# Token shift in front of the feed-forward by on-chip transfers, with new orders and banks, in a gated four-layer network on one Trainium2 core

## The chip, the cores and the metric

The kernel runs on one core of one Trainium2 chip. The metric is the time of one execution on the device in microseconds (us). The engines are TensorE (PE in the profile, its weight loads PEld), VectorE (DVE), ScalarE (ACT), GpSimd (POOL), and SyncE (SP), which issues all transfers here.

## The reference

Sixteen sequences of 128 tokens by 128 features go through four blocks of attention and feed-forward, each added with a gate. The change concerns the feed-forward of the first block, itself a transformer of six layers with local attention. One layer, for one sequence x (128 x 128):

```
x  = x + attention(shift_tokens(x))
x  = x + ffn(shift_tokens(x))
shift_tokens(t): columns 0 to 63 as they are; columns 64 to 127 of row i come from row i-1, and row 0 gets zeros

attention: qkv = x @ Wqkv (128 x 3072); 16 heads of 64
           q, k = l2norm(q) * q_scale, l2norm(k) * k_scale; both rotated by tables (cos, sin, a scale)
           scores of each window of 32 queries against its own and the previous window, times 8
           mask, softmax, @ v, @ Wo (1024 x 128)
ffn:       xn = layernorm(x) * g + b
           a, gate = split(xn @ W1 + b1)        (each 341 wide)
           (a * gelu(gate)) @ W2 + b2
```

## The kernel before

The file is written engine by engine: each engine runs its own list of instructions, in order, and waits on semaphores. Nothing is planned at run time; the orders are written out by hand.

A unit is one sequence in one layer, 6 x 16 = 96 units. Tokens lie on the 128 partitions. `local_transformer` (L445) runs three units at once in a software pipeline: each call of an engine's `stages(a, b, c)` does the first part of unit a, the middle of unit b, which is the one before, and the feed-forward of unit c, the one before that. The calls alternate between two sets of buffers (s = 0, 1). A layer is a loop of seven passes with two calls each and two calls written out behind it; between layers GpSimd also builds the rotary tables (`rotary_factors`, L1645).

The parts of a unit, in the order of its own dependences:

- `tokens` (VectorE, L2136) copies the sequence from Y to xw. `tokens_T` (TensorE, L786) transposes it, and ScalarE's `shifted` (L1299) copies the result to xsT with the shift, which is along the free dimension there.
- `queries_keys` j = 0 to 3 (L795): queries in j = 0, 1, keys in j = 2, 3, each a 128 x 512 result that fills a bank of PSUM. `values` (L816) likewise, in two halves. ScalarE squares each of the four (`squares`, L1313), VectorE sums the squares by head (`square_sums`, L2143, `floors`, L2151) and multiplies each of the four by the rotary tables (`rotated`, L2162 and L2164, two instructions). ScalarE makes inverse norms by logarithm and exponential (L1337, L1345). GpSimd adds the two products (`rotary_sum`, L1665) and multiplies by the inverse norms (`normalised`, L1679).
- `queries_keys_T` (L809, four transposes for each j) and ScalarE's copy; `scores` m = 0, 1 (L843, 64 small records each), `masked` (VectorE, L2184), `maxima` (L2192), `differences` (GpSimd, L1687), `exponentials` (ScalarE), `probs_T` (L857) and its copy, `probs_values` (L880).
- `middle_values` (SP, L532): four transfers inside on-chip memory that lay out the values for the third window.
- `inverse_sums` (L2202), `outputs` (L2209), `outputs_T` (L890), `project` (L900), `first_residual` (VectorE, L2214), which gives y1.
- `shift_back` (TensorE, L905): y1 multiplied by the identity (columns 0 to 63) and by a shift matrix (columns 64 to 127) into PSUM. `shifted_stats` and `statistics` (L2218, L2223), GpSimd's `token_var` and `token_std` (L1696, L1700), `shifted_normed` (L2227), `normed_T` (L915), `up` (L922), `gelu`, `hidden` (L2237), `down` (L934), `biased` (GpSimd, L1692), `second_residual` (L2244), which writes Y.

ScalarE loads a table of functions twice in each call, for exponentials and for the gelu. PSUM has eight banks, given to these results by the lists `lb_...` (L245 to L248); where two results share a bank, the second waits until the first is read.

## Time and profile before

| | |
|---|---|
| runs before | 2669.9, 2675.39, 2679.36 us, median 2675.39 |
| profiled execution | 2678.02 us; span from its first to its last instruction 2676.1 us |
| mean granted TensorE clock | 0.979 |
| engines busy, share of the span | TensorE 94%, weight loads 72%, VectorE 74%, ScalarE 66%, GpSimd 56% |
| instructions | 103018 |
| first L786 of the local transformer to its last | 144.0 to 1839.9 us |

The profile records one execution. A group of matmuls in order of time is merged to one row with its count: an fp32 matmul leaves two records, a transpose one. The ends of matmuls are modelled, and consecutive ones overlap in the records, so the distance from one block's start to the next block's start is what the block takes when nothing waits. Idle time in brackets is that of the engine in front of the row, with what released it.

### The profile page before, as it was taken

To read this page: it belongs to the slowest core of one execution; us is meant where nothing else is said; L and a number is where in the kernel's file an instruction comes from. 1 tells how busy PE (TensorE), PEld (TensorE's weight loads), DVE (VectorE), ACT (ScalarE), POOL (GpSimd) and SP (SyncE) were. 2 spreads that over 40 slices of the span, in tenths; PEclk is the share of its full clock that TensorE was granted. 3 is DMA by queue.
4 is the path that set the end of the run, shared out by engine and by line. 5 is a ranking of instruction groups with operands and counts; after the bars stand their busy time and mean duration, and the time that the engine had idled before them with its cause. 6 is when DMAs were issued, how large, how long until landed. Compare 5 with 4: busy or idle time off the path is not lost.

```text
span 2676.1 us, 103018 instructions
## 1 busy us (share of the span) xinstructions
PE 2507.1 (94%) x41090; PEld 1932.3 (72%) x41090; DVE 1977.9 (74%) x4815; ACT 1762.2 (66%) x3794; POOL 1492.9 (56%) x1917
## 2 busy tenths in 40 slices
PE   7879999999999999999999999999898978999898
PEld 5647677777767767777677767776677966899667
DVE  5777888888778788878788888887466877465564
ACT  5567777777777777777777777777344356333465
POOL 4567667666766766676667666775232146000472
PEclk9989999999999999999999999999799989899999
DMA  2200000111001100110011000000002000000022
GB/s 85 72 14 14 14 16 18 28 29 29 18 22 32 32 14 22 32 29 21 18 32 29 23 18 18 16 14 15 4 4 85 0 5 5 1 0 1 12 76 79
DMA packets 56280, 66.72 MB, mean 25 GB/s; under 512 B 25097, under 2 KB 30932, under 8 KB 55380
## 3 DMA queue, kind: packets, MB, share of 16 engines
q1 hardware_dynamic: 56148, 64.87, 8.7%
q8 instruction: 93, 1.52, 0.2%
q14 instruction: 39, 0.32, 0.0%
HBM read 38.23 MB, written 1.05 MB: 15 GB/s over the span
## 4 chain that ended last, share of the span: by engine, by line
PE 80%; DVE 6%; issue 5%; POOL 4%; ACT 3%; DVEq 1%; SPq 0%; POOLq 0%; DMA 0%; ACTq 0%
PE ps L795 13%; PE ps L900 6%; PE ps L816 6%; PE ps L809 6%; PE ps L880 5%; PE ps L843 5%; PE ps L922 4%; PE ps L857 3%; PE ps L1014 3%; PE ps L934 3%; PE ps L890 3%; PE ps L998 3%; PE ps L999 3%; ACT area L1190 2%; PE ps L738 2%
## 5 line engine op out<-in xcount | busy, mean ns | idle before, releaser
L1190 ACT ACTIVATE area<-ps 128x512 f32<-128x512 f32 (+3 forms) x1520 | 758.1, 532 | 415.9 <-PE ps L786 130.0
L1665 POOL TENSOR_TENSOR area<-area 128x512 f32<-128x512 f32 x384 | 482.2, 1277 | 7.9 <-DVE area L2164 7.9
L1687 POOL TENSOR_TENSOR area<-area,mx 128x512 f32<-128x512 f32 x192 | 200.2, 1043 | 491.1 <-DVE mx L2192 491.1
L795 PE MATMUL ps<-lw,area 128*128 128x512 f32 x768 | 414.1, 622 | 1.1 <-ACT area L1190 0.7
L1679 POOL TENSOR_TENSOR area<-area,rnq 128x512 f32<-128x512 f32 x384 | 393.2, 1046 | 7.5
L1313 ACT ACTIVATE area<-ps 128x512 f32<-128x512 f32 x384 | 227.4, 592 | 88.7 <-PE ps L795 88.6
L2162 DVE TENSOR_TENSOR area<-ps,table 128x512 f32<-128x512 f32 x384 | 261.0, 680 | 8.2 <-ACT area L1313 5.4
L2164 DVE TENSOR_TENSOR area<-ps,table 128x512 f32<-128x512 f32 x384 | 261.5, 681 | 0.0
L2143 DVE TENSOR_REDUCE ssq<-area 128x8 f32<-128x512 f32 x384 | 252.3, 677 | 2.4 <-ACT area L1313 1.5
L809 PE MATMUL ps<-ident,area 128*128 128x128 f32 x1536 | 218.6, 275 | 11.1 <-POOL area L1679 7.7
L809 PEld LDWEIGHTS ps<-ident,area 128*128 128x128 f32 x1536 | 180.7, 142 | 66.3 <-issue 54.3
L900 PE MATMUL ps<-lw,area 128*128 128x128 f32 x1536 | 210.2, 280 | 0.7 <-ACT area L1190 0.7
L1428 ACT ACTIVATE area<-ps 128x256 f32<-128x256 f32 x208 | 79.4, 384 | 198.8 <-PE ps L999 198.7
L880 PEld LDWEIGHTS ps<-area 64*32 64x32 f32 x9216 | 134.3, 105 | 89.7 <-issue 89.7
L900 PEld LDWEIGHTS ps<-lw,area 128*128 128x128 f32 x1536 | 186.4, 191 | 5.6 <-ACT area L1190 0.9
L816 PE MATMUL ps<-lw,area 128*64 128x512 f32 x768 | 186.0, 605 | 0.0
L843 PEld LDWEIGHTS ps<-area 64*32 64x32 f32 x12288 | 134.2, 106 | 58.7 <-issue 47.2
L2184 DVE TENSOR_TENSOR area<-ps,band_f 128x512 f32<-128x512 f32 x192 | 131.9, 687 | 59.4 <-PE ps L843 59.4
L922 PEld LDWEIGHTS ps<-xnT,lw 128*128 128x128 f32 (+1 forms) x1152 | 139.9, 180 | 48.1 <-ACT xnT L1190 46.1
L880 PE MATMUL ps<-area 64*32 64x65 f32 x9216 | 165.6, 225 | 1.2 <-issue 0.7
L843 PE MATMUL ps<-area 64*32 64x64 f32 x12288 | 165.3, 225 | 0.0
L880 PE MATMUL ps<-lvm,area 64*32 64x65 f32 x3072 | 154.0, 225 | 0.0
(301 smaller groups left out, 5681.9 us busy)
## 6 DMA issues: line engine op xcount, KB each, us to landing
lvm<-area SPq DMA_DIRECT2D x384, 65.0 KB
lw<-in_wqkv SPq DMA_DIRECT2D x36, 256.0 KB
area<-in_moe_w SPq DMA_DIRECT2D x24, 256.0 KB, 2.8
lw<-in_wout SPq DMA_DIRECT2D x12, 256.0 KB
ctxT<-in_ctxT SPq DMA_DIRECT2D x64, 38.5 KB, 1.8
lw<-in_moe_w SPq DMA_DIRECT2D x8, 256.0 KB, 2.8
lw<-in_wff SPq DMA_DIRECT2D x6, 341.0 KB
lw<-in_moe_g SPq DMA_DIRECT2D x1, 1152.0 KB
```

The costliest lines, as they stand in the source:

```text
L795: nc.tensor.matmul(banks[:, lb_qk[j], :], xsT[s], wqkv[w.p][:, j * 512:(j + 1) * 512], start=True, stop=True).then_inc(l_qk_ps, 1)
L809: last = nc.tensor.transpose(banks[:, lb_qkT[j], c * S:(c + 1) * S], QR[s][:, j * 512 + c * 128:j * 512 + (c + 1) * 128], ident[:, :])
L816: last = nc.tensor.matmul(banks[64 * odd:64 * odd + 64, lb_v[j], :].rearrange("p (c e) -> p c e", e=LD), xsT[s][:, 64 * j:64 * j + 64], he ...
L843: last = nc.tensor.matmul(banks[out_rows, lb_scores[m][odd], c * 64:(c + 1) * 64].rearrange("p (b n) -> p b n", n=WINDOW), QKT[s][64 * odd ...
L880: last = nc.tensor.matmul(banks[out_rows, lb_pv[m][odd], c * 65:(c + 1) * 65], LPT[s][rows, at:at + 32], v, start=True, stop=True)
L900: last = nc.tensor.matmul(banks[:, lb_project, 0:D], LOT[s][:, c, :], wout[w.p][:, c, :], start=(c == 0), stop=(c == 7))
L1190: return nc.scalar.activation(dst, src, ACT.Identity if kw else ACT.Copy, **kw)
L1665: pool.tensor_tensor(QR[s][:, cols], QR[s][:, cols], RA[s][:, cols], ALU.add).then_inc(l_rsum, 1)
L1679: pool.tensor_tensor(rows, rows, rnq[s][:, 8 * j:8 * j + 8, None].to_broadcast([S, 8, LD]), ALU.mult).then_inc(l_qkn, 1)
L2143: V.tensor_reduce(ssq[s][:, 8 * j:8 * j + 8], blk(SQ[s], j), AX.X, ALU.add).then_inc(l_ss, 1)
L2162: V.tensor_tensor(blk(RA[s], j), src, factors[:, 0:1, :].to_broadcast([S, 8, LD]), ALU.mult)
L2164: V.tensor_tensor(blk(QR[s], j).rearrange("p h (k e) -> p h k e", k=2), other, factors[:, 1:2, :].to_broadcast([S, 8, LD]).rearrange("p h ...
```

## The change

The shift in front of the feed-forward is done by SP: as soon as y1 of a unit is written, one transfer inside on-chip memory copies rows 0 to 126 of its columns 64 to 127 to rows 1 to 127 of 64 further columns beside it (`ysh`, whose row 0 there is set to zero once). `shifted_stats` and `shifted_normed` read the columns 0 to 63 and 128 to 191 of `ysh`. The two matmuls of `shift_back`, the shift matrix and its load go, so one load less is counted in `w1_loaded`. SP's list gets the pipeline's form. All four compute engines have a new order within `stages`, and results have other banks. The keys and queries j = 1, 3 come first, then 2 and 0; on TensorE the units' scores stand at the head of the call.

```diff
-        yb = [part(s, at_ + 1024, D) for s in bufs]
+        ysh = [part(s, at_ + 896, D + 64) for s in bufs]
+        yb = [part(s, at_ + 1088, D) for s in bufs]
...
-        lb_tokens, lb_qk, lb_qkT, lb_v = 3, (4, 3, 4, 0), (3, 0, 2, 5), (1, 5)
-        lb_scores, lb_probs, lb_pv = ((1, 2), (1, 2)), (5, 4), ((2, 3), (2, 3))
-        lb_outputs = (7, 4)
-        lb_project, lb_shift, lb_xnT, lb_up, lb_down = 7, 7, 0, (6, 7), 6
+        lb_tokens, lb_qk, lb_qkT, lb_v = 7, (3, 4, 0, 6), (4, 7, 3, 3), (2, 3)
+        lb_scores, lb_probs, lb_pv = ((6, 7), (5, 6)), (1, 4), ((4, 5), (6, 7))
+        lb_outputs = (5, 6)
+        lb_project, lb_xnT, lb_up, lb_down = 5, 1, (1, 2), 1
...
+            def shifted_tokens(s, unit):
+                sp.wait_ge(l_y1, unit + 1)
+                sp.dma_start(ysh[s][1:S, D:D + 64], y1[s][0:S - 1, 64:D]).then_inc(l_sh_ps, 16)
+            def stages(a, b, c):
+                if a:
+                    middle_values(*a)
+                    shifted_tokens(*a)
...
```

TensorE's waits that are new, and its order (b is the middle unit):

```diff
             def queries_keys(s, w, j):
                 if j == 0:
+                    follow(pe, l_v, nth(0, w.it, s, 2, 1) - 2)
...
+                if j == 3:
+                    follow(pe, l_masked, nth(0, w.it, s, 2, 1) - 2)
...
             def scores(s, w, m):
...
+                    follow(pe, l_y1, nth(0, w.it, s) - 1)
...
             def stages(a, b, c):
-                if b: queries_keys_T(*b, 1)
-                if c: shift_back(*c)
-                if a: tokens_T(*a)
-                if b: scores(*b, 0)
-                if a: queries_keys(*a, 0)
-                if b: queries_keys_T(*b, 3)
-                if a: queries_keys(*a, 1)
-                if c: normed_T(*c, b)
-                if b: scores(*b, 1)
-                if a: queries_keys(*a, 2)
...
+                if b:
+                    scores(*b, 1)
+                    queries_keys_T(*b, 2)
+                if a: tokens_T(*a)
+                if b:
+                    queries_keys_T(*b, 0)
+                    values(*b, 1)
+                    scores(*b, 0)
+                if a:
+                    queries_keys(*a, 1)
+                    queries_keys(*a, 3)
+                if c: normed_T(*c)
+                if a:
+                    queries_keys(*a, 2)
+                    queries_keys(*a, 0)
+                if b:
+                    probs_T(*b, 1, a)
+                    probs_T(*b, 0)
+                if a: values(*a, 0)
+                if b:
+                    probs_values(*b, 0)
+                    probs_values(*b, 1, a)
+                if c:
+                    up(*c, 0)
+                    up(*c, 1, a)
+                if b:
+                    outputs_T(*b, 0)
+                    outputs_T(*b, 1)
+                if a: queries_keys_T(*a, 1)
+                if b:
+                    project(*b, 0)
+                    project(*b, 1)
+                if a: queries_keys_T(*a, 3)
+                if c:
+                    down(*c, 0)
+                    down(*c, 1)
+                    down(*c, 2)
```

The new orders of the others, each shown whole in the sequence of one call (a, b, c as above):

```
ScalarE: b qkT 3, b qkT 2, a shifted, b qkT 0, load exp table, b values 1, a squares 1, b exponentials 1,
         a squares 3, c normed_T, b exponentials 0, a squares 2, b probs_T 1, b probs_T 0, a squares 0, a values 0,
         a logs and inverse norms 1, then 0, load gelu table, b outputs_T 0, c gelu 0, b outputs_T 1, c gelu 1, 2, a qkT 1
GpSimd:  b rotary_sum 1, 3, b normalised 1, 3, b rotary_sum 0, 2, b normalised 2, 0,
         c biased, c token_var, c token_std, b differences 1, 0
VectorE: a tokens, b masked 1, c shifted_stats, c statistics, b maxima 1, c shifted_normed, b masked 0, b maxima 0,
         a rotated 1, 3, a square_sums 3, 2, 1, a floors 1, a square_sums 0, b inverse_sums 0, a floors 0,
         b inverse_sums 1, b outputs 0, 1, a rotated 0, 2, c hidden 1, 0, b first_residual, c hidden 2, c second_residual
```

```diff
             def tokens(s, w):
+                follow(dve, ffn_done, nth(0, w.it, s) + G - 3)
                 follow(dve, l_y1, nth(0, w.it, s) - 2)
...
+            def shifted_tokens(s):
+                return ysh[s].rearrange("p (k n) -> p k n", n=64)[:, 0:3:2, :]
             def shifted_stats(s, w):
-                dve.wait_ge(l_sh_ps, nth(0, w.it, s))
-                V.bn_stats(st[s][:, 0:6], banks[:, lb_shift, 0:D]).then_inc(l_st, 1)
+                dve.wait_ge(l_sh_ps, 16 * nth(0, w.it, s))
+                V.bn_stats(st[s][:, 0:6], shifted_tokens(s)).then_inc(l_st, 1)
...
             def shifted_normed(s, w):
-                V.tensor_scalar(xn[s][:, :], banks[:, lb_shift, 0:D], mv[s][:, 0:1], rs[s][:, 0:1],
+                V.tensor_scalar(xn[s][:, :].rearrange("p (k n) -> p k n", n=64), shifted_tokens(s), mv[s][:, 0:1], rs[s][:, 0:1],
```

## Rows read from the trace of the kernel before

**Rows 1.** Windows: us; busy of PE, PEld, DVE, ACT, POOL; clock; DMA share; GB/s.

```profile
144.00:1839.90 1695.90, 1657.49 (x32346) 1193.96 (x32347) 1364.48 (x2922) 1305.27 (x2644) 1159.11 (x1257) 1.00 0.09 22
...
751.00:772.00 21.00, 20.88 (x350) 15.12 (x350) 14.32 (x32) 13.88 (x28) 11.13 (x12) 0.84 0.03 8
...
1255.44:1272.87 17.43, 17.43 (x344) 12.66 (x345) 14.01 (x31) 13.77 (x28) 11.43 (x13) 1.00 0.05 12
1237.07:1255.44 18.37, 17.57 (x347) 12.66 (x346) 15.06 (x32) 13.83 (x28) 12.92 (x14) 1.00 0.12 25
```

**Rows 2.** TensorE in order of time: start us, us, line, tiles, count, idle before.

```profile
1268.33 0.49 PE L934 MATMUL ps<-lw,area 85*128 85x128 f32 x2
1268.65 1.06 PE L900 MATMUL ps<-lw,area 128*128 128x128 f32 x8
...
1272.38 0.43 PE L907 MATMUL ps<-area,ident 128*128 128x64 f32 x2
...
1272.87 0.30 PE L786 MATMUL ps<-ident,xw 128*128 128x128 f32 x1
1273.10 0.86 PE L843 MATMUL ps<-area 64*32 64x64 f32 x64
1273.90 1.11 PE L795 MATMUL ps<-lw,area 128*128 128x512 f32 x2
1274.85 0.60 PE L809 MATMUL ps<-ident,area 128*128 128x128 f32 x4
1275.28 1.02 PE L795 MATMUL ps<-lw,area 128*128 128x512 f32 x2
...
1278.10 1.49 PE L922 MATMUL ps<-xnT,lw 128*128 128x128 f32 x12
...
1281.61 1.94 PE L816 MATMUL ps<-lw,area 128*64 128x512 f32 x8
```

**Rows 3.** TensorE in time at back edge and layer boundary; L786's waits (us, times).

```profile
1255.43 0.32 PE L786 MATMUL ps<-ident,xw 128*128 128x128 f32 x1 [0.80 <-DVE xw L2136]
...
1288.13 0.66 PE L809 MATMUL ps<-ident,area 128*128 128x128 f32 x4 [0.57 <-POOL area L1679]
...
  DVE xw L2136: 37.2, 32
```

**Rows 4.** VectorE's and GpSimd's timelines around two token copies.

```profile
1254.33 0.98 DVE L2136 TENSOR_SCALAR xw<-Y 128x128 f32 x1 [0.41 <-DVE area L2214]
...
1272.48 0.23 DVE L2136 TENSOR_SCALAR xw<-Y 128x128 f32 x1 [0.16 <-DVE area L2214]
...
1254.18 1.04 POOL L1679 TENSOR_TENSOR area<-area,rnq 128x512 f32<-128x512 f32 x1
...
1272.59 1.04 POOL L1679 TENSOR_TENSOR area<-area,rnq 128x512 f32<-128x512 f32 x1
```

**Rows 5.** VectorE in order of time: sums, outputs, a rotation, a mask.

```profile
1268.43 0.21 DVE L2202 RECIPROCAL rc<-ps 128x8 f32<-128x8 f32 x1
1268.68 0.69 DVE L2209 TENSOR_TENSOR area<-ps,rc 128x512 f32<-128x512 f32 x1
1269.28 0.68 DVE L2162 TENSOR_TENSOR area<-ps,table 128x512 f32<-128x512 f32 x1
...
1274.13 0.69 DVE L2184 TENSOR_TENSOR area<-ps,band_f 128x512 f32<-128x512 f32 x1 [0.47 <-PE ps L843]
```

**Rows 6.** GpSimd in order of time: three sums, and the power.

```profile
1264.52 3.75 POOL L1665 TENSOR_TENSOR area<-area 128x512 f32<-128x512 f32 x3
...
1274.01 0.55 POOL L1700 TENSOR_TENSOR rs<-ve,neghalf 128x1 f32<-128x1 f32 x1
```

**Rows 7.** Transfers: an issue in time; then KB each, us from issue to landing.

```profile
1271.78 0.51 SPq L537 DMA_DIRECT2D lvm<-area  x1
...
shift<-in_shift SPq DMA_DIRECT2D x1, 64.0 KB, 1.8
...
lw<-in_moe_w SPq DMA_DIRECT2D x8, 256.0 KB, 2.8
```

More of the change, by code:

```diff
@@ L96, in program @@
         Y = sb("Y", [S, B, D])
[L97 removed]
+        ident = sb("ident", [S, S])
         band_f = sb("band_f", [S, 2 * WINDOW])
@@ L519, in _ @@
             behind = [(dst[:, :], dram[name], w1_loaded) for dst, name in (
-                (shift, "shift"), (band_f, "band"), (heads2, "heads2"), (rank, "rank"), (aff1, "aff1"), (moe1_r, "moe1_r"))]
+                (band_f, "band"), (heads2, "heads2"), (rank, "rank"), (aff1, "aff1"), (moe1_r, "moe1_r"))]
             behind += [(dst[:, :, :], dram[name], w1_loaded) for dst, name in ((rot, "rot"), (w1, "w1"), (moe1_gu, "moe1_gu"), (moe1_d, "moe1_d"))]
-            behind[8:8] = [(dst, src, lw_loaded[p]) for p in range(2) for part in layer_parts(p, p) for dst, src in part]
+            behind[7:7] = [(dst, src, lw_loaded[p]) for p in range(2) for part in layer_parts(p, p) for dst, src in part]
             per = -(-len(behind) // (IT - 1))
@@ L538, in middle_values, with three @@
                     sp.dma_start(LVM[s][at + 32:at + 64, :, :], LV[s][at + 32:at + 64, 0, :, :]).then_inc(l_vm, 16)
-            def layer(l):
-                with sp.Fori(0, IT) as pr:
-                    for s in range(G):
-                        middle_values(s, l * B + pr * G + s)
+            def shifted_tokens(s, unit):
[5 more added lines that the diff above has]
+                    shifted_tokens(*a)
+            def three(s, unit):
+                stages((s, unit), (1 - s, unit - 1), (s, unit - 2))
             def layer_and_next_weights(l, p):
@@ L554, in layer_and_next_weights @@
                             sp.dma_start(dst, src).then_inc(lw_loaded[p], 16)
-            layer(0)
+            stages((0, 0), None, None)
+            stages((1, 1), (0, 0), None)
+            with sp.Fori(0, IT - 1) as pr:
+                for s in range(G):
+                    three(s, pr * G + G + s)
             with sp.Fori(0, DEPTH // 2 - 1) as lp:
@@ L559, in _ @@
                 layer_and_next_weights(lp * 2 + 2, 1)
-            layer(DEPTH - 1)
+            with sp.Fori(0, IT) as pr:
+                for s in range(G):
+                    three(s, (DEPTH - 1) * B + pr * G + s)
+            stages(None, (1, DEPTH * B - 1), (0, DEPTH * B - 2))
+            stages(None, None, (1, DEPTH * B - 1))
             contexts(1)
@@ L2247, in stages @@
                 if a: tokens(*a)
+                if b: masked(*b, 1)
                 if c:
@@ L2250, in stages @@
                     statistics(*c)
-                if b: masked(*b, 0)
+                if b: maxima(*b, 1)
                 if c: shifted_normed(*c)
-                if b: maxima(*b, 0)
+                if b:
+                    masked(*b, 0)
+                    maxima(*b, 0)
+                if a:
+                    rotated(*a, 1)
+                    rotated(*a, 3)
+                    square_sums(*a, 3)
+                    square_sums(*a, 2)
+                    square_sums(*a, 1)
+                    floors(*a, 1)
+                    square_sums(*a, 0)
+                if b: inverse_sums(*b, 0)
+                if a: floors(*a, 0)
+                if b:
+                    inverse_sums(*b, 1)
+                    outputs(*b, 0)
+                    outputs(*b, 1)
                 if a:
                     rotated(*a, 0)
-                    square_sums(*a, 1)
-                    rotated(*a, 1)
-                if b: masked(*b, 1)
-                if a:
-                    square_sums(*a, 0)
-                    floors(*a, 0)
-                if b: maxima(*b, 1)
-                if c: hidden(*c, 0)
-                if b: inverse_sums(*b, 0)
-                if a: rotated(*a, 2)
+                    rotated(*a, 2)
                 if c:
                     hidden(*c, 1)
+                    hidden(*c, 0)
+                if b: first_residual(*b)
+                if c:
                     hidden(*c, 2)
-                if b: outputs(*b, 0)
-                if a:
-                    square_sums(*a, 3)
-                    square_sums(*a, 2)
-                    floors(*a, 1)
-                if b:
-                    inverse_sums(*b, 1)
-                    outputs(*b, 1)
-                if a: rotated(*a, 3)
-                if c: second_residual(*c)
-                if b: first_residual(*b)
+                    second_residual(*c)
             def mixture(m):
```

266 lines of the change are left out of this document (123 added, 143 removed).

## The prediction

> **What bounds the kernel now.** I read the busy time of the engines first, then the windows, then one unit of the local transformer engine by engine in order of time. By the page TensorE is the busiest engine, at 94% of the span. The changed stage runs from the first token transpose at 144.0 us to the last at 1839.9: 1695.9 us for 95 intervals, 17.85 each, with TensorE busy 98% of it, VectorE 80% and GpSimd 68% [rows 1]. Before and behind the stage nothing is touched but one load. Two kinds of unit make the 17.85. A clean one takes 17.43 us and has no TensorE gap; the one before it takes 18.37 with 0.8 us less busy than long [rows 1]. In the clean one each block starts as soon as the one before has streamed: a block of four transposes lasts 0.60 us and the next starts 0.43 behind its start [rows 2]. There TensorE's own work sets the pace, and a block's slot is its duration less some 0.16. The 0.94 us of the other is one wait, of the token transpose for xw [rows 3], and the next view says why: the copy of the tokens (L2136) took 0.98 us there and 0.23 in the clean unit. In the slow case it started 0.15 us after a GpSimd multiplication and ended with it, 0.09 us behind; in the clean one the copy came first by 0.11 us [rows 4]. That happened at the back edge of the loop over pairs, where VectorE starts the copy 0.41 us behind the residual's end and not 0.16 [rows 4]. There are 6 x 6 back edges; the transpose waited for xw 32 times, 37.2 us in all with the pipeline's start [rows 3]. I take 30 x 0.94 = 28 us. The rest of the excess over 95 x 17.43 = 1656 is about 6 us at five layer boundaries, where the new rotary tables make GpSimd late for the transposes (0.57 us at the first block of them [rows 3]), and about 6 us at one place, where the granted clock fell to a mean of 0.84 for 21 us [rows 1]. 1656 + 28 + 12 = 1696.
>
> **What the change removes.** shift_back, two matmuls of four records: from its start to the next block 0.49 us [rows 2]. TensorE alone would then need 17.43 - 0.49 = 16.94. The orders are new too, and a block behind one of another shape, or behind a wait, costs 0.03 to 0.1 more than behind its like (the same query/key product lasts 1.11 behind the scores and 1.02 behind transposes, slots of 0.95 and 0.86 [rows 2]). Adding the blocks in the new order at their shorter starts-to-starts gives 16.6; I keep 16.5 to 16.9 as TensorE's floor. The shift matrix's load (64 KB) went beside the first stage and gives nothing.
>
> **What it adds and moves, in one unit.** Times are from u, the start of the feed-forward's up products. TensorE behind u: up 1.32, two output transposes 0.88, transposes (a,1) 0.44, project 1.80, transposes (a,3) 0.44, down 0.78, so the next stage's scores(b,1) start at 5.7 (up is 1.49 less 0.16, a half of project 1.06 less 0.16, down four records like transposes and two more, 0.33); scores 0.80, transposes (b,2) 0.44, tokens 0.23: transposes (b,0) could start at 7.2 [rows 2]. They need GpSimd's last product, and GpSimd waits for VectorE. VectorE reads the second probability product at u+0.1 (a hand-over like that from xw's end, 1255.31, to TensorE at 1255.43 [rows 3, 4]); from there it is 0.25 to outputs and then steps of 0.60 [rows 5]: outputs at 0.35 and 0.95, rotated(a,0) at 1.55 and 2.15, rotated(a,2) at 2.75 and 3.35, done at 4.05. GpSimd's sum(2) starts at 4.15 and takes 1.25 [rows 6], normalised(b,2) and (b,0) 1.04 each [rows 4] from 5.45: 6.5, done at 7.55. So transposes (b,0) start at 7.65, 0.45 late. Before, three of the four rotations stood early and one sum and one product behind the last; now the chain of two rotations, sum and two products is the bound. From there to the next u: 0.44, a half of the values 0.93, scores 0.80, two query/key products 1.81, normed 0.20, two more 1.78, probabilities' transposes 0.90, values 0.93 [rows 2], and the two probability products, as many small blocks as the scores, 1.59: 9.4. One more wait in it: queries_keys(a,3) now takes the bank of scores(b,0), so masked(b,0) (0.69 behind a hand-over of 0.24) [rows 2, 5] must fit under one product of 0.95: 0.05 to 0.1. A clean unit is 7.65 + 9.4 + 0.1 = 17.15 us, 0.28 below now. The new waits sit at the head of what is queued: behind transposes (b,0) wait all scores and products of the stage, and the masks behind those.
>
> **The transfer.** SP waits for y1 of its unit, then issues one DMA of 127 rows x 256 bytes. SP has four of its own a unit (0.51 us to issue [rows 7]) some 10 us earlier, and the next layer's weights follow behind, so nothing is ahead of it. No row has an on-chip transfer's landing. Loads of as many rows took 1.8 us (64 KB) and 2.8 (256 KB) [rows 7]; below lies the issue alone, 0.5. I take 2.0, near the 64 KB load, which is the nearest in rows and size. y1 ends at u+4.9, the rows are there at 7.0. VectorE gets to shifted_stats only behind masked(b,1), at 7.35: hidden, with 0.35 to spare. Then aggregation to 7.95, GpSimd's variance and power to 8.85 [rows 6], and masked(b,0), which cannot start before 10.05, is due after shifted_normed.
>
> shifted_normed reads and writes on-chip memory now, as the token copy does. If it goes as the copy does, it is held by a GpSimd operation that has begun: differences(b,1) starts at 8.85, as soon as the power ends, shifted_normed 0.07 behind it, and so ends 0.08 behind a 1.04 us operation [rows 4], at 9.97 and not at 9.2. That is still ahead of 10.05 and free. The Trainium skill ("SBUF — State Buffer", Who interferes with whom) has the rule: a tensor_scalar between SBUF operands can take the port pair that VectorE shares with GpSimd, exclusively, and whichever issues first makes the other block. The trace agrees for the copy [rows 4]; for shifted_normed, which read PSUM until now, no row can say. By that page the step is held; without it the step is shorter than now; the sum is the same either way, so long as 10.05 stands.
>
> **The token copy** decides the rest. second_residual starts at S+0.2 (S is the start of scores(b,1), u+5.75), the copy at S+0.65 = u+6.4. normalised(b,2) runs from 5.5 to 6.5: the copy is held to 6.6 and does no harm, since the token transpose stands behind transposes (b,2). At a back edge it starts up to 0.25 later [rows 4], 6.5 to 6.65, when normalised(b,0) has begun: held to 7.65, token transpose 7.75, transposes (b,0) at 8.0 and not 7.65 (0.35), and masked(b,1) and the statistics start 0.8 late, so that shifted_normed ends at 10.8 and masked(b,0) holds queries_keys(a,3) 0.4. Together 0.75. The rotary tables cost nothing at layer boundaries now: GpSimd has both first sums done 2 us before the inverse norms come, so the 6 us go.
>
> Sum, against the profiled span of 2676.1 (the run took 2678.0, the runs' median is 2675.4; the gain is taken from the median): 95 x 17.15 = 1629, the clock's place 6, 36 back edges x 0.75 = 27: 1662 against 1696. Gain 34, **2641 us**.
>
> **Rivals.**
> No collision at the edges (the margin is 0.1 us, my hand-overs are no better): 1635, gain 61, 2614. For it: some 6 of the 36 edges go free of it today already, with the same list of instructions.
> The GpSimd chain is hidden after all and TensorE's floor sets the pace (16.7): 95 x 16.7 + 6 = 1593, gain 103, 2572. For it: TensorE is at 98% now. Against: the chain above is 0.45 too long by rows that repeat to 0.01.
> Collision in every unit: the copy at u+6.4 need only slip 0.15 against GpSimd, then 95 x 17.9 + 6 = 1706, 2686, slower by 0.4%. It is the page's port rule at its worst; rows 4 show the price.
> The transfer's landing is on the path (ends slower): place, bn_stats in front of masked(b,0). Up to 2.4 us it is free; each further us moves the power, shifted_normed and masked(b,0), and so queries_keys(a,3), by one. At 3.1 us a unit is 17.8 and the gain is gone; at 4.0 it is 18.7, +83 us, 2758. For it: 128 rows in 256 KB took 2.8; against: 64 KB took 1.8, and this is 32 KB.
>
> **Chances.** Edges collide 0.36, none 0.27, every unit 0.14, floor 0.08, transfer late or another wait of that kind 0.15 (a third of it mild, still a gain). The likeliest is 2641, by itself 2628 to 2660. The range reaches from the side without collisions to the one with all, 2600 to 2686: that leaves out the floor and most of the late transfer. What this kernel's measurement tells from no change is about 0.3%, 8 us: faster 0.36 + 0.27 + 0.08 + 0.03 = 0.74, within 0.11, slower 0.15.
>
> **What would show it.** TensorE records a unit 340 and not 344. Waits of TensorE on GpSimd's L1679 at transposes (b,0), near 0.45 us in each unit: if none, the floor rival holds. The token copy's mean near 0.3 in odd units and 0.9 at edges, or long everywhere. shifted_normed at about 1.05 us, held, or 0.25. Period 17.15 between edges, 17.9 at them. Layer boundaries no longer visible. bn_stats waiting for a DMA would show the late transfer. The prediction is wrong if the period's floor is off the 17.15, that is, if VectorE reaches the rotations later than I think (squares on ScalarE late behind the table load), which would push everything: 0.2 us a unit are 19 us.

## The result and the profile after

After the change the kernel takes 2722.77 us (median of four runs, 2718.56 to 2726.48) where the kernel before, on the same chip, takes 2674.39 (2669.9 to 2679.36): a ratio of 1.0177, interval 1.0154 to 1.0199. It is 48 us slower, and the prediction said 34 us faster.

The windows view of the kernel after, for the whole changed stage and for one unit (columns as in [rows 1]):

```profile
143.73:1884.44 1740.71, 1639.37 (x32031) 1153.26 (x32031) 1418.18 (x2923) 1291.09 (x2644) 1167.80 (x1258) 0.99 0.09 23
1264.46:1282.61 18.15, 17.26 (x341) 12.19 (x341) 14.81 (x32) 13.61 (x29) 12.27 (x14) 1.00 0.10 25
```

The stage took 1695.9 us before and takes 1740.7 now, 18.32 a unit. TensorE works 18 us less and waits 63 more. The chain of waits says for what, in its piece from first_residual (L2236) of one unit to the query/key product (L810) behind it: start, us, what.

```profile
1334.79 0.30 DVE area L2236
1335.10 0.02 issue
1335.11 3.37 DMA area<-area
1338.49 0.02 issue
1338.51 0.31 DVE st L2243
...
1338.91 0.19 DVE mv L2248
...
1339.17 0.19 POOL ve L1715
...
1339.44 0.56 POOL rs L1719
1340.00 0.03 issue
1340.03 0.06 DVE xn L2252
1340.08 0.92 issue
1341.00 0.69 DVE area L2206
1341.69 0.04 issue
1341.74 1.12 PE ps L810 x2
```

The transfer (DMA area<-area) lands 3.37 us behind its issue, not 2.0 (3.37 to 3.73 over all 96 units, median 3.42). Everything behind it is a chain: bn_stats (L2243), aggregation, GpSimd's variance and power, shifted_normed (L2252), and behind that masked(b,0) (L2206), which frees the bank that queries_keys(a,3) takes. The timelines of the same stretch: VectorE, GpSimd and TensorE.

```profile
1338.51 0.30 DVE L2243 BATCH_NORM_STATS2 st<-area 128x6 f32<-128x128 f32 x1 [1.00 <-DMA area<-area]
...
1340.03 1.06 DVE L2252 TENSOR_SCALAR xn<-area,mv,rs 128x128 f32<-128x128 f32 x1 [0.36 <-POOL rs L1719]
1341.00 0.68 DVE L2206 TENSOR_TENSOR area<-ps,band_f 128x512 f32<-128x512 f32 x1
```

```profile
1339.96 1.04 POOL L1706 TENSOR_TENSOR area<-area,mx 128x512 f32<-128x512 f32 x1
```

```profile
1339.16 0.85 PE L863 MATMUL ps<-area 64*32 64x64 f32 x64
1339.93 1.12 PE L810 MATMUL ps<-lw,area 128*128 128x512 f32 x2
1341.74 1.12 PE L810 MATMUL ps<-lw,area 128*128 128x512 f32 x2 [0.68 <-DVE area L2206]
```

VectorE waits 1.00 us for the transfer, and shifted_normed takes 1.06 us, ending 0.09 behind the GpSimd multiplication (L1706, differences(b,1)) that runs beside it. The scores that masked(b,0) reads ended at 1340.01; it starts at 1341.00. TensorE's two pairs of L810 stand 1.81 apart where 0.95 would do. The waits view (engine, tile, line, what for: us, times, longest) says that this is every unit:

```profile
DVE st L2243 <- DMA area<-area: 57.5, 95, 2.2
PE ps L810 <- DVE area L2206: 63.1, 93, 1.0
```

### The profile page after: what moved, and what is told of

Its sections match the earlier page's. It is cut to its first block, busy times and chain, and to the rows that moved or that the text cites. A ratio compares the mean times of both kernels' runs of the same rounds, so it can differ in the third digit from the quotient of the medians.

```text
span 2722.5 us, 102526 instructions
## 1 busy us (share of the span) xinstructions
PE 2487.4 (91%) x40706; PEld 1890.1 (69%) x40706; DVE 2032.2 (75%) x4815; ACT 1747.6 (64%) x3794; POOL 1500.6 (55%) x1919
## 3 DMA queue, kind: packets, MB, share of 16 engines
HBM read 38.16 MB, written 1.05 MB: 14 GB/s over the span
## 4 chain that ended last, share of the span: by engine, by line
PE 62%; DMA 12%; DVE 10%; issue 7%; POOL 5%; ACT 3%; DVEq 0%; POOLq 0%; SPq 0%; ACTq 0%
DMA area<-area 12%; PE ps L810 10%; PE ps L920 7%; PE ps L937 6%; PE ps L900 6%; PE ps L833 4%; PE ps L910 3%; PE ps L877 3%; PE ps L1031 3%; PE ps L1015 3%; PE ps L1016 3%; DVE area L2206 2%; POOL rs L1719 2%; PE ps L824 2%; ACT area L1207 2%
## 5 line engine op out<-in xcount | busy, mean ns | idle before, releaser
L1207 ACT ACTIVATE area<-ps 128x512 f32<-128x512 f32 (+3 forms) x1520 | 769.2, 531 | 500.5 <-PE ps L824 244.4
L810 PE MATMUL ps<-lw,area 128*128 128x512 f32 x768 | 392.8, 622 | 63.9 <-DVE area L2206 63.1
L810 PEld LDWEIGHTS ps<-lw,area 128*128 128x128 f32 x768 | 124.0, 191 | 226.7 <-DVE area L2206 141.1
L1706 POOL TENSOR_TENSOR area<-area,mx 128x512 f32<-128x512 f32 x192 | 200.1, 1042 | 146.7 <-DVE mx L2214 146.5
L2165 DVE TENSOR_REDUCE ssq<-area 128x8 f32<-128x512 f32 x384 | 244.4, 678 | 8.4
L824 PE MATMUL ps<-ident,area 128*128 128x128 f32 x1536 | 238.3, 278 | 4.6 <-POOL area L1698 4.5
L833 PE MATMUL ps<-lw,area 128*64 128x512 f32 x768 | 208.5, 621 | 0.8
L920 PE MATMUL ps<-lw,area 128*128 128x128 f32 x1536 | 194.9, 280 | 0.0
L824 PEld LDWEIGHTS ps<-ident,area 128*128 128x128 f32 x1536 | 175.1, 142 | 15.4 <-POOL area L1698 6.5
L920 PEld LDWEIGHTS ps<-lw,area 128*128 128x128 f32 x1536 | 178.7, 192 | 5.2 <-ACT area L1207 0.3
L937 PE MATMUL ps<-xnT,lw 128*128 128x128 f32 (+1 forms) x1152 | 158.1, 288 | 4.9 <-issue 4.3
L900 PE MATMUL ps<-area 64*32 64x65 f32 x9216 | 156.5, 225 | 2.3 <-issue 2.2
```

What stands on the lines that cost most here:

```text
L810: nc.tensor.matmul(banks[:, lb_qk[j], :], xsT[s], wqkv[w.p][:, j * 512:(j + 1) * 512], start=True, stop=True).then_inc(l_qk_ps, 1)
L824: last = nc.tensor.transpose(banks[:, lb_qkT[j], c * S:(c + 1) * S], QR[s][:, j * 512 + c * 128:j * 512 + (c + 1) * 128], ident[:, :])
L833: last = nc.tensor.matmul(banks[64 * odd:64 * odd + 64, lb_v[j], :].rearrange("p (c e) -> p c e", e=LD), xsT[s][:, 64 * j:64 * j + 64], he ...
L900: last = nc.tensor.matmul(banks[out_rows, lb_pv[m][odd], c * 65:(c + 1) * 65], LPT[s][rows, at:at + 32], v, start=True, stop=True)
L920: last = nc.tensor.matmul(banks[:, lb_project, 0:D], LOT[s][:, c, :], wout[w.p][:, c, :], start=(c == 0), stop=(c == 7))
L937: last = nc.tensor.matmul(banks[0:hi - lo, lb_up[value], c * S:(c + 1) * S], wff1[w.p][:, at:at + hi - lo], xnT[s][:, :], start=True, stop ...
```

## The experiments

Each median stands beside runs of the kernel before on the same chip (2675.3 to 2676.3); ratios are to those. "Stage" is the distance from the first token transpose to the last, read as in the windows.

**The transfer without its last row**, so that 126 and not 127 rows move (the last token's shifted half is left out).

```diff
-sp.dma_start(ysh[s][1:S, D:D + 64], y1[s][0:S - 1, 64:D])
+sp.dma_start(ysh[s][1:S - 1, D:D + 64], y1[s][0:S - 2, 64:D])
```

> The changed kernel with one row less in the token transfer: 126 rows instead of 127 (the second half of the last token's row is not moved, so it stays what it was). Theory A: the transfer lands late (3.4 us from issue, where 2.0 was forecast) because 127 rows are sent one behind the other, and a row count with a divisor near 16 is spread over engines. Then it lands about 2.0 us behind the issue, VectorE no longer waits for it, the unit falls from 18.1-18.3 to about 17.3 us, and the time to 2625 to 2650. Theory B: any on-chip transfer with small rows takes so long, or the wait is the new order's. Then the landing stays at 3.2 to 3.4 us and the time at 2720.

2670.13, 0.9981 [0.9967, 0.9994]. One row less gives back 53 us. The transfers in one stretch of 15 us, in 40 slices of 0.375 us, GB/s of both kernels, first after, then 126 rows:

```profile
GB/s 0 0 0 0 0 0 44 0 0 0 0 0 0 0 0 0 0 18 18 18 18 14 0 0 0 0 0 44 0 0 0 0 150 28 172 50 133 116 61 0
```

```profile
GB/s 0 0 0 0 55 31 44 0 0 0 0 0 0 0 0 0 0 0 0 78 100 150 28 178 61 117 0 0 0 0 0 0 44 0 0 0 0 0 0 0
```

127 rows trickle at 18 GB/s through five slices. The packets themselves, read in both traces, say the same: of 127 rows one packet of 256 bytes starts every 0.0143 us, from 1.28 to 3.1 us behind the issue, and one engine reports the landing, at 3.5; of 126 rows all start between 1.46 and 1.73, fourteen engines report, and it has landed at 2.0. The Trainium skill ("DMA: Bandwidth & Descriptors", Why a DMA increments its semaphore by 16 and not by 1) has the rule: the number of engines is the largest up to 16 that divides the slowest dimension, for 127 partitions 1. The traces agree. I had not looked at the number of rows. The transfer has landed before VectorE asks for it, and still theory A's 17.3 and 2625 to 2650 are missed: a unit takes 17.49 and shifted_normed is still held (median 1.06). What stands behind the missing 30 us is shown in the part on why the prediction was wrong.

**127 rows as 112 and 15**, both awaited.

```diff
-sp.dma_start(ysh[s][1:S, D:D + 64], y1[s][0:S - 1, 64:D])
+sp.dma_start(ysh[s][1:113, D:D + 64], y1[s][0:112, 64:D])
+sp.dma_start(ysh[s][113:S, D:D + 64], y1[s][112:S - 1, 64:D])
```

> The changed kernel with the 127 rows in two transfers, 112 and 15. Theory A (127 rows go one behind the other): the first lands about 1.9 us behind its issue, the second about 2.5 to 2.6, since it is issued 0.6 later. That is 0.1 to 0.2 past the 2.4 that is free: a unit of 17.3 to 17.4, time 2630 to 2660. Theory B (small rows are slow as such, or the order is at fault): 2715 or more, since there is one more issue.

2685.93, 1.0035 [1.0022, 1.0047], where 2630 to 2660 were expected. A steady unit is 17.50 as with 126 rows, the landing 2.5 behind the first issue. But 44 us of the stage are in 15 long units of 18.4 to 24.3 us near the layers' starts (see below). The split cures most of the late landing, and against the kernel before the run is no gain.

**The mask in front of shifted_normed.**

```diff
-                if c: shifted_normed(*c)
-                if b:
-                    masked(*b, 0)
-                    maxima(*b, 0)
+                if b: masked(*b, 0)
+                if c: shifted_normed(*c)
+                if b: maxima(*b, 0)
```

> The changed kernel with one swap in VectorE's order: masked(b,0) in front of shifted_normed(c). The transfer stays as slow as it is. Theory A: the late transfer costs what it does because masked(b,0), on which queries_keys(a,3) waits, is queued behind shifted_normed, and that one is held 0.9 us by GpSimd's differences(b,1). With the swap queries_keys(a,3) waits under 0.2 us, a unit falls to 17.2 to 17.5 and the time to 2630 to 2660. Theory B: the late statistics delay differences and exponentials all the same, and TensorE only waits elsewhere: 2690 to 2720.

2640.48, 0.9874 [0.9856, 0.9892]: with the transfer as slow as ever, one line moved makes the kernel 82 us faster than after and 35 faster than before. The windows of its stage and one unit, and its VectorE groups (busy us, mean ns | idle before):

```profile
144.24:1802.88 1658.64, 1615.63 (x32030) 1154.30 (x32030) 1347.99 (x2923) 1283.67 (x2644) 1168.03 (x1258) 0.99 0.09 24
1177.19:1194.36 17.17, 16.99 (x341) 12.18 (x341) 14.09 (x32) 13.50 (x29) 12.29 (x14) 1.00 0.12 33
```

```profile
L2252 DVE TENSOR_SCALAR xn<-area,mv,rs 128x128 f32<-128x128 f32 x93 | 40.8, 439 | 0.0
L2243 DVE BATCH_NORM_STATS2 st<-area 128x6 f32<-128x128 f32 x93 | 27.4, 295 | 53.9 <-DMA area<-area 53.9
```

VectorE waits for the transfer nearly as long as before, and TensorE no longer waits for the mask behind it. shifted_normed, which now starts late in GpSimd's multiplication, takes 0.44 and not 1.06; unheld it takes 0.35.

**The old two matmuls of the shift**, with the new orders and banks and no transfer (result in bank 0, behind scores(b,1)).

```diff
-                    shifted_tokens(*a)
...
+                if c: shift_back(*c, b)
```

> The new orders and banks with the old shift: two matmuls (into bank 0, in front of the transposes (b,2)), no transfer, shifted_normed from PSUM and so not held. Theory A (the transfer alone is at fault, the orders are good, and the two matmuls fit in front of transposes that wait for GpSimd anyway): a unit of 17.1 to 17.3, time 2610 to 2635. Theory B (the orders cost, the transfer gains): no better than the changed kernel, 2720 or more.

2664.63, 0.9958 [0.9944, 0.9973], a unit 17.55 to 17.76. The orders and banks alone are worth 11 us, and not by a shorter clean unit (17.43 before) but because the units of 18.37 are gone. The 2610 to 2635 expected is missed. The two matmuls push transposes (b,2) back, and ScalarE's copies of them come 0.4 later, for which values(b,1) and scores(b,0) wait. That was the first sign of the third limit below.

**GpSimd's differences(b,1) behind shifted_normed**, so that it can't hold it.

```diff
+                if after:
+                    pool.wait_ge(l_xn, nth(0, after[1].it, after[0]))
```

> The changed kernel with one wait more and all orders as they are: GpSimd's differences(b,1) waits until shifted_normed(c) is done, so it cannot have begun before it. The transfer stays slow (3.4 us). Theory A (the hold by the shared port, 0.7 to 0.8 us of shifted_normed's 1.06, is the larger part of the 0.95 us that queries_keys(a,3) waits in each unit, and the late landing the smaller): shifted_normed falls to about 0.3 us, a unit from 18.07 to about 17.4, time 2650 to 2675. Theory B (the late landing is all of it, the hold is hidden): 2710 or more, and more with the differences delayed.

2660.78, 0.9942 [0.9923, 0.996], 62 us less than after with the transfer untouched; a unit 17.35 to 17.6. So landing and hold share the delay, and either alone is nearly covered: against the 17.17 of the mask in front, 3.4 with no hold costs 0.2 to 0.4 a unit, 2.0 with the hold 0.3, both together 0.95.

**126 rows and the mask in front**, and **no transfer at all and the mask in front** (the shift is left out).

```diff
-                    shifted_tokens(*a)
```

> 126 rows instead of 127 (the last token's shifted half is not moved) and masked(b,0) in front of shifted_normed(c). Theory A: with the swap alone the unit was 17.17 us and the landing no longer on the path, so a landing at 2.0 instead of 3.4 gives nothing more: 17.17, 2630 to 2650, within 8 us of the swap alone. Theory B: the statistics still cost with the swap (late differences and exponentials): 2600 to 2625.

> The swap, with no token transfer at all: SP issues none and VectorE waits for none (the shift in front of the feed-forward is left out: the second half of the statistics and the norm is over zeros). Theory A: no transfer is on the path any more with the swap, the unit stays 17.17, bound by VectorE's rotations and GpSimd's sums and products: 2630 to 2645. What may fall is the excess of some 25 us outside the steady units, if that comes from instruction fetches beside the transfers. Theory B: the transfer still costs with the swap: a unit under 17.0, 2600 to 2620.

2638.47, 0.9860 [0.9837, 0.9884], and 2636.42, 0.9851 [0.9823, 0.9879]. With the mask in front the landing is worth 2 us and the whole transfer 4, within what these runs tell apart. The long units at the layers' starts stay without any transfer.

**The kernel before, with GpSimd's normalised(b,3) behind the token copy.**

```diff
+                if after:
+                    pool.wait_ge(l_y, nth(0, after[1].it, after[0]))
```

> The kernel before with one wait more: GpSimd's last product, normalised(b,3), waits until the copy of the tokens is made, so it cannot hold it. Theory A (rows 3 and 4 were read rightly: the copy is held by GpSimd at back edges for 0.75 us and TensorE waits 0.94 for it): the copy takes 0.23 us in every unit, all units are 17.4 to 17.5 but those at layer boundaries, gain 25 to 30 us, time about 2648. Theory B (the copy is long at back edges for another reason, code that is fetched): no gain, 2670 to 2685.

2657.34, 0.9928 [0.9904, 0.9953]. The token copy's mean falls from 478 to 241 ns and the units of 18.37 are gone. It gives 18 us, not 25 to 30, as most units are now a little longer than the clean 17.43 (17.44 to 17.70), and the last unit of a layer still takes 18.69.

**Sums of squares over an eighth of the features** (j = 1, 2), with the mask in front.

```diff
+                squared = blk(SQ[s], j)[:, :, 0:8] if j in (1, 2) else blk(SQ[s], j)
```

> The kernel with the mask in front of shifted_normed, and two of the four sums of squares (j = 1, 2) taken over 8 of the 64 features of a head; the inverse norms of those two are therefore of other values, everything else is computed. VectorE's list between the second mask and outputs gets some 0.9 us shorter in a unit, TensorE's list is untouched. Theory A (a unit of 17.17 us is set by VectorE's chain: mask, rotations, sums, outputs, rotated(a,2), then GpSimd's sum, two products, transposes (b,0)): the unit falls until TensorE's own floor of 16.5 to 16.9 takes over, so 16.7 to 16.9, 25 to 45 us less than the kernel with the mask in front, 2595 to 2615. Theory B (TensorE's own work is the 17.17 and my floor of 16.5 to 16.9 was too low): 17.17 stays, 2640, within 8 us.

2639.47, 0.986 [0.9836, 0.9883], the unit 17.17. Theory A falls as it stood: VectorE's new idle time appears in front of the second reciprocal (0.49 where it was 0.34), which waits for TensorE anyhow.

**The old matmuls with the mask in front** (both edits above together).

> The new orders and banks, the mask in front of shifted_normed, and the old two matmuls of the shift in place of the transfer. Against the kernel with the mask in front and the transfer (2640.5) this is what the transfer itself is worth once its landing is off the path. Theory A (VectorE's chain sets the unit, and TensorE has 0.3 to 0.5 us to spare ahead of it): the 0.49 us of the matmuls are mostly covered, 2640 to 2655. Theory B (TensorE sets the unit): 0.49 x 95 = 47 us more, 2680 to 2690. A third figure lies between, from the kernel with the matmuls and the mask behind (2664.6): where the mask's place gives nothing without a late landing, 2660 to 2668.

2666.01, 0.9962 [0.995, 0.9974]. The same as with the mask behind: its place does not matter where shifted_normed reads PSUM, and so is not held (0.40 to 0.41 us in every unit), and waits for no transfer. Between two kernels with the mask in front, transfer for matmuls is worth 25.5 us, of 0.49 x 95 = 47.

**Two of GpSimd's sums halved** (j = 0, 2; the other halves keep the first product), and **the token copy on ScalarE**.

```diff
-                cols = slice(j * 512, (j + 1) * 512)
+                cols = slice(j * 512, j * 512 + (256 if j in (0, 2) else 512))
```

```diff
+                copy(xw[s][:, :], Y[:, w.pr * G + s, :]).then_inc(l_y, 1)
...
                     queries_keys_T(*b, 3)
+                if a: tokens(*a)
+                if b: queries_keys_T(*b, 2)
```

> The mask in front of shifted_normed, and GpSimd's sums j = 0 and 2 taken over 256 of their 512 columns (the others keep the first product alone, so queries and keys of those are of other values). The short sums of squares took away time of VectorE ahead of the second probability product, where VectorE waits 0.3 us for TensorE anyhow; this takes time away behind it. Theory A (a loop sets 17.17 us: second probability product, outputs, rotated(a,0), GpSimd's two sums 2.51 and two products 2.04, token copy and transposes (b,0), TensorE's blocks from there to the second probability product): the two sums take 1.2 to 1.3 us less, the loop's slack of TensorE in front of transposes (b,0), 0.35 us, goes first, and a unit takes 16.8 to 16.9; 25 to 35 us less than 2640, so 2605 to 2615. Theory B (TensorE's own blocks are 17.17): 2640, within 8.

> The mask in front of shifted_normed, and the token copy made by ScalarE between its copies of transposes (b,3) and (b,2), where it is idle for 1.6 us, in place of VectorE. On VectorE the copy ended 0.08 us behind GpSimd's last product in every unit, so the token transpose (0.17 us) stood between that product and transposes (b,0). Theory A (held by the port that VectorE shares with GpSimd, and on the loop): ScalarE's copy takes 0.3 to 0.4 us, the token transpose is done before GpSimd's product ends, and the unit falls by 0.15 to 0.2 us from 17.17 to 17.0; 15 to 19 us less than 2640, so 2620 to 2626. Theory B (the copy is not on the loop): the unit stays 17.17, 2640. Theory C (ScalarE's copy waits for GpSimd as well, or the residual's hand-over to ScalarE eats the gain): 2635 to 2650, the copy's duration would show it.

2645.09, 0.988 [0.9864, 0.9897], and 2639.54, 0.9871 [0.9853, 0.989]. ScalarE copies the tokens in 0.31 us beside a GpSimd product, not held. In both the wait in front of the token transpose goes (0.3 with the mask alone, under 0.1 here), and the unit stays 17.1 to 17.3: values(b,1) and scores(b,0) start later instead. Theory A missed twice, so something else has the same length.

**A bank of its own for transposes (b,2)** (0 for 3): alone, with the token copy on ScalarE, and with the halved sums too.

```diff
-lb_qkT = (4, 7, 3, 3)
+lb_qkT = (4, 7, 0, 3)
...
                 if j == 1:
-                    pe.wait_ge(l_qkT, nth(0, w.it, s, 4, 2))
+                    pe.wait_ge(l_qkT, nth(0, w.it, s, 4, 1))
```

> The mask in front of shifted_normed, and transposes (b,2) in bank 0 and not 3, so that values(b,1), which takes bank 3, need not wait for ScalarE to copy them. Theory A (two limits of nearly one length: GpSimd's products with the held token copy, and behind them this bank): the waits of 0.09 and 0.09 behind transposes (b,0) go, the one in front of the token transpose stays; a unit of 17.17 becomes 16.98 to 17.05, 2622 to 2632. Theory B (the bank is hidden behind GpSimd's products): 17.17, 2640.

> The same with the token copy on ScalarE. Theory A: transposes (b,0) start 0.12 us behind GpSimd's last product, the token transpose in front of them: 16.85 to 16.95 a unit, 2612 to 2620. Theory B (neither is the limit, TensorE's own blocks are): 17.1, 2635 to 2640.

> The same, and GpSimd's sums j = 0 and 2 taken over 256 of their 512 columns (queries and keys of the others keep the first product alone). Theory A: nothing stands in front of transposes (b,0) and values(b,1) any more, and what is left is TensorE's own floor by its starts-to-starts, 16.6 to 16.75: 2590 to 2603. Theory B: as the run before, within 8.

2641.97, 0.988 [0.9863, 0.9897]; 2641.04, 0.9868 [0.9846, 0.9891]; 2637.51, 0.9863 [0.9847, 0.988]. Nothing moves. In the third, values(b,1) follows at once, and now the scores behind it wait. Its TensorE and ScalarE:

```profile
1194.27 0.66 PE L824 MATMUL ps<-ident,area 128*128 128x128 f32 x4
...
1195.40 1.08 PE L833 MATMUL ps<-lw,area 128*64 128x512 f32 x4
1196.72 0.85 PE L863 MATMUL ps<-area 64*32 64x64 f32 x64 [0.24 <-issue]
```

```profile
1194.96 1.66 ACT L1207 ACTIVATE area<-ps 128x512 f32<-128x512 f32 x4 [0.53 <-PE ps L824]
```

ScalarE makes four copies in a row: transposes (b,2), the two halves of the shifted tokens, transposes (b,0). They start 0.03 behind the end of the first of these and the scores start 0.10 behind their end. From transposes (b,2) to scores(b,0) it is 2.45 here, and in all of these kernels 2.45 to 2.50.

**The shifted tokens behind the copy of transposes (b,0)**, which wants the token transpose in bank 0 and transposes (b,2) in 7: alone, with the token copy on ScalarE, and with the halved sums too.

```diff
-                if a: shifted(*a)
                 if b: queries_keys_T(*b, 0)
+                if a: shifted(*a)
```

> The mask in front of shifted_normed. ScalarE copies transposes (b,0) ahead of the shifted tokens; for that the token transpose goes to bank 0 and transposes (b,2) to bank 7, and values(b,1) does not wait for their copy. Theory A (ScalarE's four copies in a row set the distance of 2.47 from transposes (b,2) to scores(b,0)): that limit falls to 1.98, and what is left is GpSimd's last product with the held token copy in front of the transposes, so transposes (b,0) and values(b,1) follow without waits: 17.17 becomes 17.0 to 17.1, 2626 to 2636. Theory B (something else): 17.17, 2640.

> The same with the token copy on ScalarE. Theory A: GpSimd's last product ends 7.37 us behind u, transposes (b,0) start at 7.5 and take 0.44, values(b,1) 0.93, and from scores(b,0) to the next u it is 7.95: a unit of 16.8 to 16.9, 25 to 35 us less than 2640, 2606 to 2616. Theory B: 17.1, 2635 to 2640.

> The same, and GpSimd's sums j = 0 and 2 over 256 of their 512 columns (the other queries and keys keep the first product alone). Theory A: TensorE's own floor, 16.6 to 16.75: 2590 to 2603. If GpSimd was not the limit of the run before: no difference to it, within 6. Theory B: 17.1, 2635 to 2640.

2635.46, 0.9853 [0.9835, 0.9872]; 2630.87, 0.9832 [0.9814, 0.9851]; 2623.46, 0.9799 [0.978, 0.9818]. The signs are those of theory A and the sizes are smaller: the steady units are 17.17, 16.8 to 17.1, and 16.81 to 16.97. The first reaches its 2626 to 2636, but its steady unit is that of theory B, and 5 us are little beside the runs' spread; the second and third miss theory A's times. The banks of two results move with the order in these three, which no run separates; the bank of transposes (b,2) alone moved nothing. The second computes everything and is the fastest such kernel of the study, 45 us under the one before. The windows of the second and the third, their stages:

```profile
144.40:1794.24 1649.84, 1612.52 (x32031) 1159.50 (x32031) 1303.69 (x2828) 1306.97 (x2738) 1167.69 (x1257) 0.99 0.10 24
```

```profile
144.23:1785.39 1641.16, 1603.20 (x32031) 1159.91 (x32032) 1312.62 (x2828) 1305.78 (x2738) 1070.34 (x1258) 0.99 0.10 25
```

## Why the prediction was wrong

**The transfer's landing: the step that failed.** "I take 2.0, near the 64 KB load, which is the nearest in rows and size." It took 3.4. The load had 128 rows and so did the 256 KB one; 127 rows go over one engine and 126 over fourteen. The number of rows decided, not the bytes. A nearer row would not have helped: the four transfers of the values' windows, on-chip ones of 32 rows each, land in 2.0 in the profile after. Of the 82 us between 2641 and the 2723 measured, this step is 53, by the run with 126 rows.

**The rival "the transfer's landing is on the path"** is what happened, with a chance of a tenth. Its total fits: by its rule, free up to 2.4, then one for one, 3.37 makes a unit 17.15 + 0.97 = 18.12, and measured are 18.05 to 18.4. Its steps don't. With a landing at 2.0 and at 2.5 the unit is 17.5 and not 17.15 to 17.25, and from there the late landing adds 0.6, not 1.0. That the two errors add up to 18.12 is luck. (Its 83 us for a landing at 4.0 are 87 by its own unit of 18.7.) 95 x 18.12 + 6 = 1727 against 1740.7; the rest is mostly in seven units, 15.3 us above the median together.

**shifted_normed in front of the mask: a second step that failed.** Held to 1.05 by differences(b,1): right (median 1056 ns). "That is still ahead of 10.05 and free": wrong, with a landing in time too. With 126 rows, moving the mask to the front takes the unit from 17.49 to 17.17 and the time from 2670.13 to 2638.47. One unit with 126 rows and the mask behind, TensorE and then VectorE; u is 1148.36:

```profile
1148.36 1.59 PE L937 MATMUL ps<-xnT,lw 128*128 128x128 f32 x12
...
1154.31 0.85 PE L863 MATMUL ps<-area 64*32 64x64 f32 x64
...
1157.58 0.86 PE L863 MATMUL ps<-area 64*32 64x64 f32 x64
1158.37 2.31 PE L810 MATMUL ps<-lw,area 128*128 128x512 f32 x4
1160.51 0.27 PE L927 MATMUL ps<-ident,xn 128*128 128x128 f32 x1
```

```profile
1154.95 0.87 DVE L2158 TENSOR_SCALAR xw<-Y 128x128 f32 x1 [0.16 <-DVE Y L2271]
1155.74 0.68 DVE L2206 TENSOR_TENSOR area<-ps,band_f 128x512 f32<-128x512 f32 x1
1156.34 0.28 DVE L2243 BATCH_NORM_STATS2 st<-area 128x6 f32<-128x128 f32 x1
...
1157.84 1.05 DVE L2252 TENSOR_SCALAR xn<-area,mv,rs 128x128 f32<-128x128 f32 x1 [0.36 <-POOL rs L1719]
1158.81 0.68 DVE L2206 TENSOR_TENSOR area<-ps,band_f 128x512 f32<-128x512 f32 x1
```

The token copy ends at u+7.46 where the prediction had 6.6, and masked(b,1) and the statistics queue behind it. So shifted_normed starts at u+9.48 and ends at 10.53, not 9.97. The scores are done at 10.08, and masked(b,0) starts only at 10.45. The two products of L810 last 2.14 to the next block, where they take 1.82 without a wait: that is the 0.3. Unheld, at 0.35 us, shifted_normed would have ended at 9.83 (an estimate), so the late copy and the hold are both needed. That division is read from the rows; no run has the landing in time and only one of the two taken away. With the late landing, taking away the hold gives 62 us.

**The token copy at the back edges, 27 us: wrong.** The copy was held in nearly every unit. In a layer's steady part it takes 0.84 to 0.88 between the edges and 0.46 to 0.62 at them, where it starts 0.4 later, and it ends 0.08 behind GpSimd's second product in both. So no unit is longer for an edge: in the first and the last layer they take 18.05 to 18.08 in a row, in the others 18.1 to 18.2 up to an edge and mostly 18.2 to 18.4 behind it. The 27 us are not there. The miss is in the starts. scores(b,1) start at u+5.95 and not 5.75 (the up products alone take 1.44 to the next block and not 1.32), so the copy begins at u+6.6 and not 6.4, while GpSimd's second product begins at 6.33 and not 6.5. The 0.15 that the rival "collision in every unit" asked for was there. It had the place right and the price wrong, 0.75 a unit: with the mask behind, the copy's hold is one of the two causes of the 0.3 above; with the mask in front it costs 0.17, the token transpose that is pressed between GpSimd's last product and transposes (b,0), and ScalarE's copies hide even that. The kernel with the mask in front: GpSimd's two products at an edge, then VectorE's copy between the edges and at one, TensorE and ScalarE at that edge:

```profile
1192.18 2.04 POOL L1698 TENSOR_TENSOR area<-area,rnq 128x512 f32<-128x512 f32 x2
```

```profile
1176.26 0.87 DVE L2158 TENSOR_SCALAR xw<-Y 128x128 f32 x1 [0.16 <-DVE Y L2271]
...
1193.76 0.54 DVE L2158 TENSOR_SCALAR xw<-Y 128x128 f32 x1 [0.49 <-DVE Y L2271]
```

```profile
1193.63 0.66 PE L824 MATMUL ps<-ident,area 128*128 128x128 f32 x4
1194.36 0.33 PE L799 MATMUL ps<-ident,xw 128*128 128x128 f32 x1
1194.53 0.60 PE L824 MATMUL ps<-ident,area 128*128 128x128 f32 x4
1195.06 1.08 PE L833 MATMUL ps<-lw,area 128*64 128x512 f32 x4
1196.08 0.85 PE L863 MATMUL ps<-area 64*32 64x64 f32 x64
```

```profile
1194.32 1.66 ACT L1207 ACTIVATE area<-ps 128x512 f32<-128x512 f32 x4 [1.63 <-PE ps L824]
```

GpSimd is done at 1194.22, the copy at 1194.30; the token transpose and transposes (b,0) follow without a gap. ScalarE's four copies end at 1195.98 and the scores start at 1196.08.

**The clean unit, 17.15: right in size, once the mask stands in front** (17.17 to 17.26), and only half right in cause. transposes (b,0) start 7.68 behind u (1186.85 in this unit), as worked out (7.65): GpSimd's product ends 0.18 earlier than I had it, and the token transpose takes the difference. But two limits of nearly one length stand there: that chain, and ScalarE's row of copies, 2.45 to 2.50 from transposes (b,2) to scores(b,0) where TensorE's own blocks between them take 1.98. My sum had no term for ScalarE. Taking away the first alone gave nothing (two runs), the second alone 5 us, both some 10 and with the halved sums 17. That 2640 with the mask in front is also the 2641 predicted is luck: the 27 us at the edges are not in it, and some 25 us of long units that the prediction did not have are (below).

**TensorE's floor, 16.5 to 16.9: right.** With all of it out of the way the shortest units are 16.81, and TensorE is busy for 16.80 of one that takes 16.84.

**The wait of queries_keys(a,3) for masked(b,0), 0.05 to 0.1**: nothing with the mask in front, where the two products (four records) take 1.82 together.

**The layer boundaries, 6 us to be gained: not gained.** The long last unit of a layer (18.67 before) is gone, as forecast, but long units of 18 to 22 us stand among a layer's first four instead, with no transfer as well; many are the unit that ends at the loop's first way back. In the kernel with the mask in front the stage is some 25 us above 95 steady units, in the one with the split transfer 44. TensorE's waits there, of 1 to 4.5 us, are mostly put down to "issue", to nothing that the profile shows. Instructions being fetched would fit, as the lists are other code from layer to layer; that wasn't tried, and the cause stays open.

The clock adds to them. In the fastest kernel the granted clock falls to its lower level, 1.2 GHz, six times between 170 and 1794 us, 23.9 us in all; five of the falls come right behind a TensorE stall of 1.7 to 2.1 us. With the mask alone it is three times, 10.2 us, two of them behind such stalls. The one left over, near 735 to 740 us, has no stall before it and stands in both. One long unit of the fastest kernel, the stretch at the lower clock in it, and a steady unit:

```profile
1035.05:1055.90 20.85, 18.77 (x342) 13.89 (x341) 13.76 (x31) 13.91 (x29) 12.80 (x15) 0.92 0.07 16
1047.90:1051.30 3.40, 3.40 (x18) 3.40 (x17) 3.03 (x6) 1.18 (x3) 1.49 (x2) 0.50 0.00 0
1140.64:1157.71 17.07, 16.96 (x342) 12.18 (x341) 13.78 (x31) 13.88 (x29) 12.35 (x14) 1.00 0.12 33
```

The same 342 records keep TensorE busy 1.8 us longer, and the stall itself is 2.0. It is also why the fastest kernel's unit, 0.2 us shorter than that with the mask alone, gives 10 us and not 20: its stage is 1649.8 us where 95 x 16.98 would be 1613. Of the 12 us by which this excess is larger, some 7 are the clock (an estimate: half of 23.9 - 10.2).

## What to carry to other kernels

Before a transfer is costed, look at the count of its slowest dimension: 127 rows cost 1.4 us more than 126. Put what waits for a transfer behind whatever the busiest engine waits for; here one moved line was worth 82 us, and curing the landing as well only 2 more, which the runs' spread does not tell from none. When an operation is forecast to fit ahead of another by 0.1 us, work out what is queued in front of it too: here a copy that ended 0.9 us later than forecast undid it. Where a shorter chain moves nothing, look for a second one of the same length before blaming the engine: here GpSimd's chain and ScalarE's four copies hid each other.

## What was not expected of the hardware

A transfer between partitions of 127 x 256 bytes landed 3.4 us behind its issue and one of 126 rows 2.0. GpSimd's differences, which stand in its list right behind the power, started 0.07 us before VectorE's shifted_normed, which waits for the same power, in 94 of the 96 units, so that VectorE's is held for all of it (1.06 for what takes 0.35 unheld). A ScalarE copy between on-chip buffers is not held (0.31 beside a GpSimd product, where VectorE's took 0.46 to 0.88). And a TensorE stall of some 2 us can cost nearly as much again, when the granted clock falls behind it.
